# Two transformer blocks with mixtures of experts on one core: last batch's layer-norm statistics ahead of a barrier that leaves out the scatter's sends

## The reference

```python
mod = (silu(c) @ wmod).reshape(B, 6, 1, -1)
sa, ca, ga, sb, cb, gb = mod[:, 0], ..., mod[:, 5]      # ga, gb: magnitude at least 0.25
h = layernorm(x) * (1 + ca) + sa
x = x + ga * attention(h)
h = layernorm(x) * (1 + cb) + sb
x = x + gb * mixture(h)
```

```python
scores = softmax(xf @ gate_w.T)                  # 2048 tokens x 32 experts
weights, indices = top_k(scores, 4)
# per token: the 4 picked experts, silu(x w1) * (x w3) @ w2, weighted
# plus one shared expert of hidden size 256 for every token
y = sum_e w_full[:, e] * expert_e(xf) + shared(xf)
```

## Time and profile before

| | us |
|---|---|
| median of 3 runs | 1425.9 |
| lowest, highest | 1424.57, 1441.39 |
| profiled execution | 1425.93 |
| its span, first to last instruction | 1424.6 |
| TensorE busy | 1280.9 (90%) |
| VectorE busy | 870.1 (61%) |
| ScalarE busy | 783.5 (55%) |
| GpSimd busy | 457.3 (32%) |

### The profile page before, as it was taken

How to read it: one execution, slowest core, us unless ns; L and a number is a source line. 1 busy time by engine, 2 the same in 40 slices (tenths; PEclk the granted TensorE clock), 3 DMA queues, 4 the chain that set the end, 5 groups by cost and what they waited for, 6 DMA issues and landing times.

```text
span 1424.6 us, 22581 instructions
## 1 busy us (share of the span) xinstructions
PE 1280.9 (90%) x6461; PEld 906.7 (64%) x6461; DVE 870.1 (61%) x2637; ACT 783.5 (55%) x1919; POOL 457.3 (32%) x589
## 2 busy tenths in 40 slices
PE   6589998887799998799999999999999977999994
PEld 5334443335456776577777777787877754677773
DVE  5668887754652365665577567756676755433555
ACT  3268675663432445676667666665666643166552
POOL 5344644220435644200010025001500150455553
PEclk9679999997999999899999999999999997999997
DMA  7732616215113553044100001000100019455764
GB/s 218 143 79 56 120 49 138 78 35 217 58 41 115 158 155 103 33 149 153 56 1 1 16 8 53 1 16 1 53 9 16 1 57 365 163 154 154 209 200 132
DMA packets 79207, 133.99 MB, mean 94 GB/s; under 512 B 13788, under 2 KB 52708, under 8 KB 77420
## 3 DMA queue, kind: packets, MB, share of 16 engines
q1 hardware_dynamic: 62128, 92.39, 20.7%
q0 software_dynamic: 15712, 38.25, 10.0%
q10 hardware_dynamic: 1248, 1.90, 0.4%
HBM read 77.20 MB, written 60.00 MB: 96 GB/s over the span
## 4 chain that ended last, share of the span: by engine, by line
PE 66%; DVE 14%; issue 7%; ACT 5%; DMA 5%; POOL 4%; SPq 0%; DVEq 0%; ACTq 0%; POOLq 0%
PE psum L126 8%; PE psum L128 7%; PE psum L127 7%; PE psum L2008 7%; PE psum L2658 7%; PE psum L2704 5%; PE psum L2531 4%; PE psum L1979 3%; PE psum L854 3%; PE psum L883 3%; PE psum L2565 2%; DVE psum L1943 2%; DVE a_nmax L790 2%; PE psum L2627 1%; PE psum L778 1%
## 5 line engine op out<-in xcount | busy, mean ns | idle before, releaser
L790 DVE TENSOR_REDUCE a_nmax<-psum 128x2 f32<-128x1024 f32 x128 | 154.9, 1215 | 56.6 <-PE psum L778 55.5
L1954 ACT ACTIVATE a_spare<-psum,a_nmax 128x128 f32<-128x128 f32 (+3 forms) x256 | 134.7, 526 | 90.9 <-DVE a_nmax L1943 82.2
L869 ACT ACTIVATE a_et<-psum 128x512 f32<-128x512 f32 x256 | 139.0, 594 | 81.2 <-PE psum L854 77.5
L2727 POOL DMA_INDIRECT results<-r_fin,r_to x134 | 134.3, 1002 | 123.5 <-ACT r_fin L2719 60.6
L2008 PE MATMUL psum<-a_et,a_v 128*128 128x512 f32 (+3 forms) x512 | 169.9, 434 | 1.8 <-DVE a_ctx L2025 1.6
L1943 DVE CUSTOM_DVE_ANT_0 psum<-psum,a_spare 128x128 f32<-128x128 f32 (+3 forms) x256 | 127.1, 496 | 63.0 <-PE psum L128 56.5
L2658 PE MATMUL psum<-m_w,m_xT 128*128 x536 | 150.4, 403 | 0.0
L1988 ACT ACTIVATE a_et<-psum 128x128 f32<-128x128 f32 (+3 forms) x256 | 111.4, 435 | 44.6 <-PE psum L1979 42.0
L126 PE MATMUL psum<-a_kT,a_q 128*128 128x128 f32 (+3 forms) x256 | 118.8, 464 | 6.6 <-DVE a_q L1882 5.9
L854 PE MATMUL psum<-a_stk 50*128 50x512 f32 x256 | 105.8, 480 | 18.4 <-ACT a_et L869 12.3
L1979 PE MATMUL psum<-ident,a_spare 128*128 128x128 f32 x640 | 113.2, 275 | 1.0 <-DVE a_spare L1967 1.0
(11 more groups left out here) (329 smaller groups left out, 3007.8 us busy)
## 6 DMA issues: line engine op xcount, KB each, us to landing
r_xs<-slots SPq DMA_DIRECT2D x134, 129.0 KB, 2.3
slots<-empty SPq DMA_DIRECT2D x12, 1290.0 KB, 6.0
m_w<-in_experts SPq DMA_DIRECT2D x16, 768.0 KB, 14.3
stacks<-a_qk SPq DMA_DIRECT2D x32, 256.0 KB, 3.7
a_stk<-stacks POOLq DMA_DIRECT2D x32, 256.0 KB, 5.1
r_shared_hid<-results SPq DMA_DIRECT2D x12, 512.0 KB, 4.8
m_w<-in_experts SPq DMA_DIRECT2D x4, 1216.0 KB, 14.2
a_stk<-stacks POOLq DMA_DIRECT2D x32, 128.0 KB, 5.7
```

The source lines that it names most:

```text
L790: dve.tensor_reduce(nmax[:, G % 2, qt, 2 * p:2 * p + 2], psum[:, n:n + 2, :], AX.X, ALU.max, negate=True).then_inc(s_max.sem, 1)
L869: act.activation(et[:, n % NET, 2 * p + hh, :], psum[:, 4 + hh, :], ACT.Exp).then_inc(s_e.sem, 1)
L1954: act.activation(e[:, u % NE, 0:W], psum[:, n, 0:W], ACT.Exp, bias=nmax[:, u % NE, :], scale=-1.0, accum_out=rsum[:, u % NE, :]).then_inc( ...
L2727: pool.indirect_dma_start(results[:, :], bass.IndirectOffsetOnAxis(ap=to[:, i % NI, 0:1].bitcast(U32), axis=0), ys[:, o, :], None, bounds_ ...
```

## The change

Four edits. At the end of `attention1`, behind its loop, batch 3's four `bn_stats`, four `bn_aggr`, the root and the five small operations are emitted, with one square root of the constant `eps` into a one-column tile on ScalarE ahead of them. The block ahead of `mixture`'s loop that did the same work is gone. The barrier at L3068 leaves out the semaphores that begin with `dma_send`. The row buffer is allocated by the caller, on the right side of the on-chip memory, where it lives until the end of the program, and is handed to `attention1`. The sends stay in the list of the barrier that ends the second mixture.

```diff
-def attention1(k, weights, norm, gate_rows, front):
+def attention1(k, weights, norm, gate_rows, front, rows):
...
         front.work(weights.stage[:, :, :].rearrange("p a b -> p (a b)"), 
-                   [sb("rows", [P, K1, ROW])[:, :, :]])
+                   [rows])
...
+        sqrt_warm = sb("sqrt_warm", [P, 1])
...
             scalar(s)
             vector_late(s)
             gpsimd(s)
+        for t in range(TT):
+            norm.vector_stat((B - 1) * TT + t, t)
+        act.activation(sqrt_warm[:, :], k.eps[:, :], ACT.Sqrt).then_inc(k.sem("act_warm").sem, 1)
+        k.sem("act_warm").up()
+        norm.vector_mean_var(range(TT))
+        norm.at = slice(0, TT)
+        norm.scalar_sd()
+        norm.vector_rstd()
...
-            if done:
-                norm.vector_stats(range(done * TT, (done + 1) * TT))
-                norm.scalar_sd()
-                norm.vector_rstd()
             for t in range(TT):
                 norm.vector_xn(done, t, t)
...
-            attention1(k, weights, norm, gate_rows, front)
-        k.barrier()
+            rows = k.sb(stack, "a1_rows", [P, K1, ROW], side="right")[:, :, :]
+            attention1(k, weights, norm, gate_rows, front, rows)
+        k.barrier("dma_send")
```

## The result

| | before | after |
|---|---|---|
| median, us | 1431.07 | 1423.84 |
| lowest, highest | 1417.79, 1442.85 | 1412.48, 1432.83 |
| runs | 20 (the three shown first among them) | 20 |
| profiled execution | 1425.93 | 1426.98 |
| its span | 1424.6 | 1425.7 |

The ratio is 0.995, with a 95% interval of 0.9928 to 0.9972: the change gains about 7 us of 1431, a small gain but one clear of the scatter; by the interval it is 4.0 to 10.3 us. Forecast was 1419.6 us, in a range of 1416.3 to 1423.5. The time came out 0.3 us above that range, although the ratio forecast (1419.6 / 1425.93 = 0.9956) is nearly the one measured. That the two ratios come so close is in part luck, since the interval is 6 us wide. The two profiled executions, set side by side, even have the changed kernel 1.05 us slower. So the whole span cannot show this change, and the seam can.

A forecast was written before the change was run, and what follows sets the result against it. At the seam between second attention and second mixture, the scatter's wait, then statistics and table load, were taken as the bound. The tile 6.67 us earlier, less 0.3 for the clock, took 1425.93 to 1419.6 us; range 1416.3 to 1423.5.

The forecast's parts named there:

- The base: Whole kernel: the profiled execution's 1425.93 us matches the median of three runs, 1425.9, so sums need no shift.
- The barrier without the sends: Barrier between second attention and second mixture: without the sends it costs 0.14 to 0.55 us, taken as 0.14.
- Rival 1: Second seam: the barrier still ends with the scatter, only the moved work is hidden; gain 4.55, 1421.4 us, chance 0.06.
- The statistics ahead: Second seam: batch 3's statistics run beside the scatter, no shorter; root at 1174.02, small operations done at 1175.36.
- A root for the table: ScalarE at the second seam: an early root loads the table while ScalarE idles, taking 1.28 us off the path.
- VectorE beside GpSimd: Second seam: a small operation or first tile could wait up to one send's length; the trace's pairing did not agree.
- What has to keep up: Loads behind the second seam's barrier: each loses 4.5 us of cover, but cover is left everywhere, 1.3 us at the thinnest.
- Rival 4: Loads behind the second seam's barrier: a late first kept batch delays the shared matmuls; 1428.3 us, chance 0.03.
- The clock: TensorE behind the second seam: the clock still falls and rises later, 0.3 us lost; bounds 2.0 gained, 1.9 lost.
- Rival 3: Front behind the second seam: TensorE's clock stays up throughout, a further 4.7 us gained, 1414.9 us, chance 0.05.

The follow-up runs named there:

- e1: Changed kernel with the sends kept in the barrier's list, statistics and early root still ahead of it; median 1420.71 us, ratio 0.9941 to the kernel before.
- e2: Changed kernel with statistics, root and small operations back behind the barrier and no early root, sends still left out; median 1427.29 us, ratio 0.9972.
- e3: Changed kernel without the early square root that only loads ScalarE's table; seam 4.63 us instead of 3.41, 1436.72 us in one run.
- e10: Repeat of e5, the changed kernel with 16 unused TensorE matmuls at the seam, on another chip; median 1423.25 us over six runs.
- e11: The changed kernel itself, unedited, run again on another chip beside the kernel before; median 1424.26 us over six runs, ratio 0.9955.
- e7: Changed kernel with three transfers of expert weights issued ahead of the kept batches instead of behind them; 1436.38 us in one run.
- e6: Changed kernel with e5's 16 unused matmuls and three more between the front's transposes and the router's matmuls; median 1430.23 us, ratio 0.9947.
- e9: Changed kernel with one unused full-size matmul ahead of each pair of score matmuls in the first attention's last batch; median 1453.90 us, ratio 1.0136.
- e5: Changed kernel with 16 unused matmuls on TensorE behind the second attention's last transposes, to keep its clock up; 1423.78 us in one run.

## Why the prediction was right or wrong

**The base: the step that failed.** The prediction said that the profiled execution (1425.93) and the median of the three runs (1425.9) agree, "so sums made against it need no shift". Both were draws from a wide scatter. Of the 20 runs of the kernel before, 6 lie at or below 1425.9, and the median is 1431.07; the further sets of 25 and of 11 gave 1430.92 and 1431.21, and one of 13 gave 1440.01. The highest of the three, 1441.39, was taken for an outlier ("which a median of few runs seldom shows"), but 1442.85 and 1439.66 came again. Beside the later profiles of the same code (first seam at 330.4 to 352.2 us) its own 334.83 is an early one; the profile alone could not tell that, but three runs 17 us apart were a warning. With 1431.07 for a base the same sum gives 1431.07 - 6.67 + 0.3 = 1424.7, and 1423.84 was measured. So the step that failed is the base with the range put round it, not the term for the change.

**The barrier without the sends: right.** It costs 0.21 us from the last small operation to the tile, where 0.14 less an overlap was taken. Rival 1 (it still ends with the scatter) is what e1 looks like, with 5.53 us of seam, and the changed kernel's is 3.41.

**The statistics ahead: right to 0.02 us.** From x's end to the root 1181.33 - 1179.50 = 1.83 us (forecast 1.85), to the end of the small operations 3.20 (3.19). The seam's gain of 6.56 stands against 6.67. That it is no sum of its parts is shown by e1 and e2.

**A root for the table: right.** Predicted were 1.28 us, e3 shows 1.22. On what the Trainium skill says in "ScalarE: Activation LUTs", section "What ACT_TABLE_LOAD costs", that a switch comes to about 2.66 us with its drain: in the changed kernel the load starts at 1173.43, 0.02 us behind ScalarE's last activation, and the root follows at 1174.72, so the trace again has 1.29 and doesn't agree.

**VectorE beside GpSimd: nearly nothing, but not nothing.** The statistics took 1.40 us beside the sends, 1.41 without them. Of the small operations one, L335, took 0.23 instead of 0.16 in the changed kernel's first profile. Eight later profiles show more. In them L339, which takes 0.17 with no send beside it, starts 0.51 to 0.64 us behind the last send, takes 0.30 to 0.42 and ends 0.93 or 0.94 behind the send's start, so as its issue (0.96) ends. Where it started 0.43 or 0.50 behind (the first profile and e10), it took 0.17. GpSimd's and VectorE's rows of e11:

```profile
1169.68 0.96 POOL L1636 DMA_INDIRECT slots<-a_rows,f_slot_of  x1 [0.31 <-issue]
```

```profile
1170.19 0.42 DVE L339 TENSOR_SCALAR ln_work<-ln_work 128x4 f32<-128x4 f32 x1
```

So a small operation can wait up to 0.25 us for the rest of a send, and that is most of what parts e11's seam of 3.60 from 3.41. The Trainium skill, "SBUF — State Buffer", section "Who interferes with whom", says that of a VectorE operation in a two-port mode and a GpSimd instruction the later one waits until the other is over. The rows agree with that for the second half of a send only, if L339 runs in such a mode, which no row shows. The prediction's row of 1153.81 starts 0.14 us behind its send and ends too early to meet that part. Two microseconds before it, beside a copy of GpSimd's, the same line took 0.87 us, and nearby on 128x512 0.48 or 0.49:

```profile
1151.42 1.04 POOL L1605 COPY a_rows<-a_spare 128x1024 f32<-128x1024 f32 x1 [1.59 <-DMA slots<-a_rows,f_slot_of]
```

```profile
1151.87 0.87 DVE L1967 TENSOR_SCALAR a_spare<-a_spare,a_rinv 128x512 f32<-128x512 f32 x1
```

**What has to keep up: right, and thin.** The first kept batch is issued at 1184.23, lands 5.4 us later at 1189.6 and is wanted at 1192.56: 2.9 us of cover, where the worst case of 1.3 was named. e7 shows a wait once it lands later, and e6 once the front is 1.9 us faster and SyncE starts 0.6 us later. Rival 4 (the loads decide) did not come about.

**The clock: right in sum, wrong in cause.** Forecast was a loss of 0.3 us, from a later rise. By its own working (half of a delay of 0.3) that term should have been 0.15. The front did take 0.26 us more, but the rise came as before (2.4 us behind the first shared matmul against 2.5); the loss is ScalarE's 0.31 us ahead of `h_m`. That 0.26 is near 0.3 is luck. Rival 3 (the clock stays up) did not come about: it fell at 1181.3, ahead of the transposes at 1183.47.

## What to carry to other kernels

Before a change of half a per cent is weighed, the base needs as many runs as its scatter asks for, and a single profile is placed within that scatter by a landmark ahead of the change (here the first seam), once several profiles show where such landmarks fall; the time between two landmarks then shows what whole spans hide. Work that doesn't depend on what a barrier waits for belongs ahead of it, its table load too, but such gains are set by the later of two chains and do not add. Once a wait is shortened, the loads issued behind the same barrier are next in line, and their cover should be read off before more is taken out.

## What was unexpected of the hardware

- The same code ended the first attention between 330.4 and 352.2 us, with a granted clock of 0.94 to 0.70 from 240 to 330 us (e9 aside), and whole executions of either kernel spread over 20 us and more.
- On two of the four chips ScalarE and VectorE stood still near the end of the last front in every profile (VectorE's wait ahead of `m_w_at` 3.0 to 5.1 us, elsewhere 1.5), though TensorE's records show their matmuls done. In all seven profiles VectorE goes on 0.3 to 0.9 us behind SyncE's first fetch of sorted rows, which waits for the last sends (1222.03 and 1222.81 in e5, 1231.12 and 1231.99 in e6); on the other two chips it is 5.4 to 5.5 us ahead of it. What stops them isn't shown.
- One instruction more or less in ScalarE's stream moved a later write of that stream by 0.31 us.
- An operation of VectorE on 4 columns took 0.42 instead of 0.17 us when it started in the second half of GpSimd's issue of an indirect DMA.
